# First layer's softmax denominators by all-ones matmuls a step apart, with reciprocals in eight pieces, 18 of a batch's blocks summed by ScalarE, and another order of the copies at a batch's turn

## What is computed

```
scores = jnp.einsum('bhtd,bhsd->bhts', q, k) / scale
attn = jax.nn.softmax(scores, axis=-1)
out = jnp.einsum('bhts,bhsd->bhtd', attn, v)
x = x + out.transpose(0, 2, 1, 3).reshape(B, T_text, N_HEADS * HEAD_DIM) @ Wo
```

## Time and profile before

| | us |
|---|---|
| median of 3 runs (2175.75 to 2176.48) | 2175.83 |
| the profiled execution, its own time | 2174.4 |
| its span, first to last instruction | 2172.6 |

### The profile page before, as it was taken

One profiled execution on the slowest core, in us unless ns is written; L12 is line 12 of the kernel. 1 busy time (PEld: TensorE's weight loads), 2 busy tenths in 40 slices (PEclk: granted clock), 3 DMA queues, 4 the chain that ended last, 5 costly groups with the idle time before them and its releaser, 6 DMA issues. The chain is left out here.

```text
span 2172.6 us, 27566 instructions
## 1 busy us (share of the span) xinstructions
PE 2110.9 (97%) x8962; PEld 1571.2 (72%) x8962; DVE 1575.4 (73%) x2592; ACT 972.9 (45%) x2593; POOL 1409.9 (65%) x1120
## 2 busy tenths in 40 slices
PE   7999999999999999999999988999999999999999
PEld 7777777777777777777777556666666666665998
DVE  4889888898889888988896642556665666652677
ACT  3444445545454445444545337544444344431432
POOL 1468776887778777877787237187878787771221
PEclk9999999999999999999999999999999999999999
DMA  3000000000000000000001410011011111101110
GB/s 132 29 15 16 29 29 15 21 23 29 15 29 15 29 19 25 15 29 29 15 10 40 140 46 1 29 43 57 29 57 30 56 49 37 43 1 52 37 52 25
DMA packets 15136, 75.63 MB, mean 35 GB/s; under 512 B 1746, under 2 KB 2114, under 8 KB 13986
## 3 DMA queue, kind: packets, MB, share of 16 engines
q1 hardware_dynamic: 14994, 73.89, 10.4%
HBM read 72.97 MB, written 0.92 MB: 34 GB/s over the span
## 5 line engine op out<-in xcount | busy, mean ns | idle before, releaser
L612 POOL TENSOR_TENSOR l_prod<-l_prod 125x256 f32<-125x256 f32 x576 | 417.4, 738 | 270.4 <-DVE l_prod L677 269.7
L677 DVE TENSOR_TENSOR l_prod<-l_side,xq 125x512 f32<-125x512 f32 x576 | 394.9, 686 | 56.2 <-PE l_side L809 48.3
L954 POOL TENSOR_TENSOR l_acc<-l_acc,l_probs 125x896 f32<-125x896 f32 x160 | 346.0, 2162 | 81.7 <-ACT l_probs L904 66.0
L553 ACT ACTIVATE l_probs<-l_slots,mask_bias 125x448 f32<-125x448 f32 x384 | 237.8, 632 | 340.6 <-PE l_slots L748 340.5
L974 DVE TENSOR_TENSOR l_scaled<-l_slots,rk 125x896 f32<-125x896 f32 x192 | 207.0, 1085 | 197.8 <-PE l_slots L1039 197.7
L606 POOL TENSOR_TENSOR l_acc<-l_acc,l_probs 125x896 f32<-125x896 f32 x160 | 338.6, 2116 | 0.0
L535 ACT ACTIVATE l_prod_act<-l_prod_act 125x128 f32<-125x128 f32 x768 | 228.0, 298 | 235.3 <-DVE l_prod_act L677 235.3
L904 ACT ACTIVATE l_probs<-l_scaled 125x896 f32<-125x896 f32 x192 | 182.8, 952 | 320.7 <-DVE l_scaled L974 296.8
L686 DVE TENSOR_REDUCE l_msq<-l_prod 125x4 f32<-125x256 f32 x576 | 235.0, 410 | 1.7
L640 DVE SCALAR_TENSOR_TENSOR top<-l_side,mask_bias,top 125x448 f32<-125x448 f32 x330 | 223.4, 677 | 6.8 <-PE l_side L792 5.8
L1037 PE MATMUL l_slots<-l_qhi,l_clo 128*125 128x448 f32 x384 | 203.0, 529 | 1.4 <-DVE l_qlo L979 1.4
(11 more groups left out here) (258 smaller groups left out, 4487.9 us busy)
## 6 DMA issues: line engine op xcount, KB each, us to landing
land<-in_ctxT SPq DMA_DIRECT2D x32, 750.0 KB, 4.3
l_nat<-in_ctxN SPq DMA_DIRECT2D x16, 750.0 KB
post_we<-in_experts SPq DMA_DIRECT2D x20, 384.0 KB, 3.0
spare<-in_ctxN SPq DMA_DIRECT2D x8, 750.0 KB
nat<-in_ctxN SPq DMA_DIRECT2D x8, 750.0 KB
spare<-in_wo SPq DMA_DIRECT2D x2, 2048.0 KB, 8.5
spare<-in_wqT SPq DMA_DIRECT2D x4, 512.0 KB, 9.2
mid_fac<-in_factors SPq DMA_DIRECT2D x1, 2048.0 KB, 8.2
```

Of the source, the lines that this page charges most:

```text
L553: act.activation(P[t % NP][:, HALF * i:HALF * i + HALF], bank_of("S", t, i)[0:KT, 0:HALF], ACT.Exp, bias=m.mask_bias[:, b, t:t + 1]).then_ ...
L612: pool.tensor_tensor(buf[:, :, 0:C // 2], buf[:, :, 0:C // 2], buf[:, :, C // 2:C], ALU.add).then_inc(s.half_sum, 1)
L677: dve.tensor_tensor(to[:, :, :], bank, xt.unsqueeze(1).to_broadcast([KT, 4, C]), ALU.mult).then_inc(s.side_dve, 1)
L954: pool.tensor_tensor(acc[:, :], acc[:, :], P[t % NP][:, :], ALU.add).then_inc(s.acc, 1)
```

## The change

The denominators: `sums` becomes one float32 matmul of 448 columns for each half, with a matrix of ones as weights, so that the sums come out on all 128 partitions. The first half stands in step 0, the second at the start of step 1. `spread` is gone. ScalarE copies each half out of PSUM (`sums_out`), VectorE takes reciprocals of 112 columns on 128 partitions, one in each of steps 2 to 9 behind the fourth side job (`invert`), and GpSimd multiplies in steps 7 and 11 (`normalise`). GpSimd also makes `shift` now, at the start of step 10.

The blocks: 30 `N` and 18 `A` a batch in place of 36 and 12, with four buffers for `N` in place of five, and strings that put the first `M` behind an `N`.

The batch's turn: the exponentials of tile 0 come first, then `nat_high`, the queries' rounding, the first quarter of the context's rounding, `values_out`, `norms_out` and the other three quarters.

```diff
-NPROD, NPROD_ACT, LAG_N, NLOW = 5, 2, 3, 4
-NBLK = NT * DVE_G
+NPROD, NPROD_ACT, LAG_N, NLOW = 4, 2, 3, 4
+BLOCKS_N = [(t, g) for t in range(NT) for g in range(3 - t % 2)]
+BLOCKS_A = [(t, g) for t in range(NT) for g in range(3 - t % 2, NG)]
-STEPS = ["MNMNM", "MNAMNMN", "NMNAMNNM", "NMANMNM", "NMNAMNNM", "NMNAMNM", "ANMNNMN", "NNMANMN", "NAMNNMA", "NTANTNN", "ANNA", ""]
+STEPS = ["NMNMM", "MNAMNMAN", "NMANMNAM", "MNAMNMAN", "NMANMNAM", "MNAMNMA", "NAMNMAN", "MANMNA", "MANMNAN", "TANTNAN", "NNN", ""]
...
-ORDER = [("S", 0, 0), ("S", 0, 1), ("S", 1, 0), ("S", 1, 1), ("D", 0, 0), ("E", 0, 0), ("E", 0, 1)]
+ORDER = [("S", 0, 0), ("S", 0, 1), ("S", 1, 0), ("S", 1, 1), ("D", 0, 0), ("D", 0, 1), ("-", 0, 0)]
...
+            def sums_out(b, half):
+
+                act.wait_ge(s.den, 2 * b + half + 1)
+                need(act, s.o_done, 2 * b)
+                act.activation(den[:, half, :], bank_of("D", 0, half)[:, 0:HALF], ACT.Copy).then_inc(s.den_out, 1)
...
                 for t in range(NT):
-                    if t == NT - 1 and b + 2 < B:
-                        high_parts(b + 2)
+                    if t == 1 and b > 0:
+                        sums_out(b - 1, 1)
                     for tile in tile_ahead(1, b, t):
                         exp(*tile)
+                    if t == 0 and b > 0:
+                        sums_out(b - 1, 0)
+                    if t == NT - 1:
+                        if b + 1 < B:
+                            nat_high(b + 1)
+                        if b + 2 < B:
+                            query_high(b + 2)
+                            context_high(b + 2, 0)
...
                 values_out(b)
                 norms_out(b)
-                if b + 1 < B:
-                    nat_high(b + 1)
+                if b + 2 < B:
+                    context_high(b + 2, 1)
...
+            def normalise(b, half):
+
+                pool.wait_ge(s.o_raw, b + 1)
+                pool.wait_ge(s.inv, QBLK * b + 4 * half + 4)
+                o = m.qs[:, b, :, :].rearrange("p (a h) q -> p a (h q)", a=2)[:, half, :]
+                pool.tensor_tensor(o, o, den[:, half, :], ALU.mult).then_inc(s.o_done, 1)
...
                 for t in range(NT):
+                    if t == 10 and b + 1 < B:
+                        make_shift(b + 1)
                     if t > 0:
                         add(b, t)
+                    if b > 0 and t in (7, 11):
+                        normalise(b - 1, t // 11)
...
+            def invert(b, j):
+
+                dve.wait_ge(s.den_out, 2 * b + j // 4 + 1)
+                part = den[:, j // 4, TT * (j % 4):TT * (j % 4) + TT]
+                dve.reciprocal(part, part).then_inc(s.inv, 1)
...
-                    for n in jobs:
+                    for at, n in enumerate(jobs):
                         side_job(n)
+                        if at == 3 and b > 0 and 2 <= t < 2 + QBLK:
+                            invert(b - 1, t - 2)
...
-                for j in range(QBLK):
-                    last = pe.matmul(out[:, 0:TT], m.row_of[0:KT, 127 - j:255 - j], acc[:, TT * j:TT * j + TT],
-                                     start=j == 0, stop=j == QBLK - 1)
-                last.then_inc(s.den, 1)
...
+                wait_bank(pe, b + 1, "D", 0, half)
+                pe.matmul(bank_of("D", 0, half)[:, 0:HALF], m.ones[0:KT, :], acc[:, HALF * half:HALF * half + HALF],
+                          start=True, stop=True).then_inc(s.den, 1)
```

More of the change, by code:

```diff
@@ L58, in plan @@
                 STEP_JOBS[b, t].append(add("V", b))
-    assert all(made[kind, b] == (n if kind in "NA" or b > 0 else 0) for b in range(B) for kind, n in zip("MTNA", (2 * NT, 2, NBLK, NT)))
+    assert all(made[kind, b] == (n if kind in "NA" or b > 0 else 0) for b in range(B) for kind, n in zip("MTNA", (2 * NT, 2, NBLK, NBLK_A)))
 plan()
@@ L433, in first_attention @@
         "ld_land", "ld_nat0", "ld_nat1", "ctx_hi", "ctx_lo", "q_hi", "q_lo", "nat_hi", "xq", "shift",
-        "scores", "probs", "pv", "acc", "den", "inv", "spread", "o_raw", "o_done",
+        "scores", "probs", "pv", "acc", "den", "den_out", "inv", "o_raw", "o_done",
         "ld_wv", "ld_wo", "side_pe", "side_dve", "side_act", "half_sum", "sum_dve", "sum_act", "rk_pre"])
@@ L453, in first_attention @@
         msq = sb("msq", [KT, NT, H], F32)
+        den = sb("den", [C, 2, HALF], F32)
         side = [psum(f"side{i}", [128, 512]) for i in range(3)]
@@ L474, in wait_bank @@
                 if kind == "D" and b > 0:
-                    return pe.wait_ge(s.inv, b)
-                if kind == "E" and b > 0:
-                    return pe.wait_ge(s.o_done, 2 * b - 1 + half)
+                    return pe.wait_ge(s.den_out, 2 * b - 1 + half)
                 at -= 3
@@ L511, in _, with query_high, context_high @@
         def _(act):
-            def high_parts(b):
+            def query_high(b):
+                need(act, s.scores, 2 * NT * (b - 1))
+                act.activation(qhi[b % 2][:, :], m.qs[:, b, :, :].rearrange("p h q -> p (h q)"), ACT.Copy).then_inc(s.q_hi, 1)
+            def context_high(b, part):
                 need(act, s.ld_land, 16 * (b - 1))
@@ L517, in high_parts @@
                     act.wait_ge(s.side_pe, last_of(b - 2, "NA") + 1)
-                act.activation(chi[b % 2][:, :], land[:, :], ACT.Copy).then_inc(s.ctx_hi, 1)
-                act.activation(qhi[b % 2][:, :], m.qs[:, b, :, :].rearrange("p h q -> p (h q)"), ACT.Copy).then_inc(s.q_hi, 1)
+                cols = slice(0, S // NLOW) if part == 0 else slice(S // NLOW, S)
+                act.activation(chi[b % 2][:, cols], land[:, cols], ACT.Copy).then_inc(s.ctx_hi, 1)
             def nat_high(b):
@@ L534, in add_up @@
                     whole = prod_act[at % NPROD_ACT][:, c, :]
-                    last = act.activation(whole, whole, ACT.Copy, accum_out=msq[:, t, 12 + c:13 + c])
+                    last = act.activation(whole, whole, ACT.Copy, accum_out=msq[:, t, 4 * g + c:4 * g + c + 1])
                 last.then_inc(s.sum_act, 1)
@@ L578, in _ @@
                 norms_out(b)
-                if b + 1 < B:
-                    nat_high(b + 1)
+                if b + 2 < B:
+                    context_high(b + 2, 1)
+            for half in range(2):
+                sums_out(B - 1, half)
         @block.gpsimd
@@ L625, in _ @@
                             halve(n)
+            for half in range(2):
+                normalise(B - 1, half)
         @block.vector
@@ L730, in _ @@
                             add_up(b, i)
-            invert(B - 1)
-            normalise(B - 1)
+            for j in range(QBLK):
+                invert(B - 1, j)
         @block.tensor
@@ L759, in values_half, with sums @@
                     last.then_inc(s.pv, 1)
[L761 removed]
+            def sums(b, half):
                 pe.wait_ge(s.acc, (NT - 1) * (b + 1))
[L764 to L780 removed]
+                wait_bank(pe, b + 1, "D", 0, half)
+                pe.matmul(bank_of("D", 0, half)[:, 0:HALF], m.ones[0:KT, :], acc[:, HALF * half:HALF * half + HALF],
+                          start=True, stop=True).then_inc(s.den, 1)
             def side_job(n):
@@ L823, in _ @@
                     if t == 1 and b > 0:
-                        spread(b - 1)
+                        sums(b - 1, 1)
                     for half in range(2):
@@ L834, in _ @@
                     side_jobs(len(jobs))
-            sums(B - 1)
-            spread(B - 1)
+            for half in range(2):
+                sums(B - 1, half)
 def second_attention(nc, m, a, tag, sem):
```

77 lines of the change are left out of this document (26 added, 51 removed).

## The result

The changed kernel takes 2165.27 us in the median of five runs (2164.04 to 2165.41); five runs of the kernel before gave 2175.75 (2174.36 to 2176.48). The ratio is 0.9951, with an interval of 0.9936 to 0.9965: 10.5 us faster. The profiled execution's own time is 2165.27, its span 2163.5 (before 2174.4 and 2172.6). 31.8 were forecast, and the time lies outside the predicted range, 3 us above its upper end.

The account below looks back on a forecast made before the run. TensorE was taken to bound the kernel. 14 x (2.08 + 1.73 - 1.2 - 0.3) = 32.3, plus 1.8 for the fifteenth turn, 1.0 start, -3.3 end: 31.8 us off 2175.83 gives 2144.0, range 2125 to 2162.

Parts of the forecast that it names:

- What TensorE saves: Denominators, each batch: dropping `sums` and `spread` (1.79 us each) for two float32 matmuls (1.50) saves TensorE 2.08 us.
- The old waits of the turn: Batch's turn: first `M` waiting for `qhi` and third `M` for VectorE's reciprocal and `xq` both vanish; 1.73 us, 14 times.
- The turn's new waits: Batch's turn: GpSimd's addition may stretch `xq` from 1.68 to 3.2 us; costed at nothing, 0.5 a turn if VectorE later.
- `acc`: Sums of step 0 wait for GpSimd's chain to the denominators: 0.3 us a batch taken, bounds 0 to 1.
- VectorE in steps 2 to 4: Steps 2 to 4: VectorE needs 6.5 us a step, TensorE 6.1; costs TensorE 1.2 us a batch, bounds 0 and 3.
- Start and end: First layer's attention: earlier first exponentials win 1.0 us at the start; the longer chain after the last sums loses 3.3.
- Behind the end: Stages after the first layer's attention: the forecast had no term for them and counted no change.
- (b): Rival: VectorE bounds most steps, or a turn wait stays; 3.2 us of waits a batch, 2160 to 2170, chance 0.18.
- The rule of the page: Batch's turn: by the skill's rule on SBUF blocking between VectorE and GpSimd, `xq` would be held in every turn.

Follow-up runs that it names:

- the nine matmuls: The changed kernel with nine unread float32 matmuls of 448 columns added on TensorE behind the last sums of the first layer's attention: 2161.25 us.
- the kernel with the old end: The changed kernel with only the last batch's denominators made as before the change (eight 112-column matmuls, one reciprocal, `spread`, VectorE's multiplications): 2158.46 us.
- the kernel before with the new split: The kernel before with only the 30 `N`, 18 `A` and new strings of the change, first job still `M`: 2163.78 us.

## Why the prediction was wrong

By the place where the next stage starts, 14.6 us were won ahead of it (1217.74 to 1203.16) where 31.8 were forecast, and 5.4 were lost behind it, where nothing was.

**What TensorE saves: right.** 2.08 a batch forecast, 2.07 by the distances between starts.

**The old waits of the turn: one gone, with the reason in doubt, the other not.** "So I take both waits as gone: 1.73 a turn". The first `M` waits for nothing, and no row waits for `qhi`. I gave this to the new order of the copies; the new numbers and order of the blocks do it without them. But the `M` that waited for `l_prod` waits for it still, 13 times, now since VectorE is late with `xq` and no longer with the reciprocal as well.

**The turn's new waits: this step failed.** "I cost this at nothing, and at 0.5 a turn if VectorE is a microsecond later than I think", and 0.3 for `acc`. Measured were 1.50 in place of 0.3. The mechanism was named, but its size was taken from one meeting of two instructions: "up to 3.2", which no row gives but which one instruction in the way nearly bears out (2.95 to 3.34), became 4.41, since a second GpSimd instruction stood directly behind the first. I stopped at the addition, though the printed order of the streams had the multiplication in the very next row. With `xq` held by one instruction 0.90 a turn comes back, with `shift` off GpSimd 1.27. A batch came out at 70.17 in place of 71.27 - 2.31 = 68.96; these 1.21 in each of 13 batches are 15.7 of the 17.2 us missing ahead of the next stage; batch 1, with only one instruction in the way at its turn and `acc` in time, came out 0.15 off.

**`acc`:** 0.5 a turn at the ones-matmul's start, 0.6 with the row behind it, 0.3 forecast, within the bounds of 0 to 1. GpSimd's `shift` took 1.69 where I used 2.08. The chain is nevertheless late, and taking `shift` out of it ends the wait: the balance of 9.8 against 9.8 was too close for a value at the low side.

**VectorE in steps 2 to 4: right.** 1.2 a batch forecast, 1.25 measured; each reciprocal 0.84, a full row 0.71 (5.83 for eight, the last to its end), forecast 0.85 and 0.72. Taking them away and adding six sums moved the waits as this step says.

**Start and end.** The wait of the earlier trace rows fell to 0.19, so 1.2 was won in place of 1.0, of which 0.5 was given back because the stage itself started later in this execution (75.96 in place of 75.48):

```profile
75.96 0.44 PE L772 MATMUL l_slots<-qhi,clo 128*125 128x448 f32 x1 [1.10 <-PEq L160]
79.30 0.47 PE L772 MATMUL l_slots<-qhi,clo 128*125 128x448 f32 x1 [0.19 <-ACT l_probs L557]
```

From the sums to the next stage 9.2, forecast 9.3. With the waits of the fifteenth turn and of the last batch's steps, everything behind the start of batch 15's second step misses 1.1.

**Behind the end: this term was put at nothing, without a reason.** I counted 3.3 us of a longer chain and didn't ask what TensorE's clock does while it stands idle in it. Of the 5.4 us lost there, the nine matmuls brought back about 4. What makes the later falls is explained in part. The first of them stands in all ten kernels at the end of 3.1 us in which TensorE waits for GpSimd; the kernel before has the same wait, and no fall:

```profile
1276.52 0.61 PE L1407 MATMUL mid_bk<-mid_sql,mid_one_r 128*128 128x448 f32 x1 [3.16 <-POOL mid_sql L1250]
```

```profile
1288.50 0.47 PE L1393 MATMUL mid_bk<-mid_sql,mid_one_r 128*128 128x448 f32 x1 [3.14 <-POOL mid_sql L1236]
```

Why the clock falls beside the one and not beside the other stays open, as does the fall at 1310 us. In the kernel with the old end the clock is at the lower level for 6.8 us from 1269.8, without any fall ahead of it, and in the kernel before with the new split, whose end is that of before, for 3.4 us from 1276.5 and again from 2017.2 (958.2 behind the end, 3.3 more than before). So part of the 5.4 need not come from the idle 7.4 us.

**Which rival it was.** (b), "one of the turn's waits stays", gave 2160 to 2170 at 3.2 us of waits a batch; measured are 2.8 and 2165.3, and of its two conditions it is the second that holds. It had 0.18. The prediction says that its range reached to the middle of (b); that would be 2165, and its upper end of 2162 is not. The kernel came out at that middle. That the time fits is in part luck: (b) too has nothing for the 5.4 us behind the end.

**The rule of the page.** The Trainium skill (SBUF — State Buffer, "Who interferes with whom") said that a VectorE instruction with two SBUF inputs and a GpSimd instruction that reads SBUF block each other for their whole length, and I wrote that by it "`xq` would be held in every turn". The rows agree: 1.76 when GpSimd is idle, 2.96 to 4.42 beside it, and the GpSimd instruction behind it held in return. It was used for the row of the addition only; followed through the whole list of GpSimd's instructions there, it would have shown that 4.41 is possible. It doesn't decide between that and 3.3: the page has whoever issues first get the ports, and by the starts printed here that would be `xq`. In 13 turns the rows show otherwise.

## What to carry to other kernels

When work moves to another engine, lay the two engines' instruction lists side by side at the point where they meet, and add up *all* that can stand in the way of the one on the path, not only the first. An engine that is 79% busy (GpSimd here, 55.5 of 70.15 us) had no room at the turn. An engine's idle time inside a chain has a price beyond its length: look at what the next stage does behind it, and at the clock. And try each part of a large change alone: here the new numbers and order of the blocks gave as much as the whole, while two other parts, moved elsewhere, gave another 18.6 and 13.0 us.
